# Fetching codewords by indirect DMA in place of a one-hot matmul, in a four-layer convolution kernel

## What is computed

```python
x = jnp.transpose(inputs, (0, 2, 3, 1))
flat = x.reshape(-1, 32)
distances = jnp.sum(flat * flat, axis=1, keepdims=True) + jnp.sum(codebook * codebook, axis=1) - 2.0 * flat @ codebook.T
indices = jnp.argmin(distances, axis=1)
quantized = codebook[indices].reshape(input_shape)
quantized = x + jax.lax.stop_gradient(quantized - x)
```

## Time and profile before

| | |
|---|---|
| median of 3 runs | 2005.93 us (1997.58 to 2012.52) |
| span of the profiled execution | 1997.8 us |
| busy: PE / DVE / ACT / POOL | 83% / 73% / 61% / 59% of the span |
| scoring stage of group 4 | 1034.1 to 1112.8 us |
| scoring stage of group 0 | 151.3 to 222.3 us |

### The profile page before, as it was taken

The page is one execution under the profiler, slowest core; times in us unless marked ns, Lnnn a source line. Parts: engine busy times, 40 slices in busy tenths (PEclk is TensorE's granted clock), DMA queues, the critical chain, the costliest instruction groups (busy, mean ns, idle before and its releaser), DMA issues.

```text
span 1997.8 us, 48789 instructions
## 1 busy us (share of the span) xinstructions
PE 1651.5 (83%) x18498; PEld 1357.9 (68%) x18498; DVE 1465.0 (73%) x3147; ACT 1213.4 (61%) x1819; POOL 1176.1 (59%) x1578
## 2 busy tenths in 40 slices
PE   0238657989889898888989898898989898898999
PEld 0113346668856787668856797668866797668998
DVE  3147647887779877797769777787768866797776
ACT  0003245667657675667757585666757576677986
POOL 4000036677657756577657666577657765577764
PEclk9965578999989998999989899899989998999999
DMA  8944396469755796459955696558955696235542
GB/s 146 216 112 137 82 209 172 137 172 228 201 140 182 179 221 180 143 161 225 224 149 163 168 236 194 143 160 211 217 162 145 179 229 178 62 86 144 152 143 84
DMA packets 286788, 333.16 MB, mean 167 GB/s; under 512 B 215664, under 2 KB 225904, under 8 KB 282332
## 3 DMA queue, kind: packets, MB, share of 16 engines
q1 hardware_dynamic: 240856, 228.88, 44.5%
q0 software_dynamic: 28176, 80.41, 16.5%
q10 hardware_dynamic: 17524, 20.75, 3.5%
HBM read 256.45 MB, written 60.09 MB: 158 GB/s over the span
## 4 chain that ended last, share of the span: by engine, by line
PE 52%; DVE 15%; DMA 7%; issue 6%; ACT 5%; SPq 5%; DVEq 4%; POOL 3%; ACTq 2%; POOLq 0%
PE bank L1353 28%; PE bank L1452 6%; PE bank L1340 4%; SPq L453 4%; DMA lent<-z_rows 3%; PE bank L1437 3%; DVE code L1215 3%; PE bank L1410 2%; PE bank L1337 2%; DVEq L1214 2%; PE bank L1322 2%; DVE onehot L1222 2%; PE bank L1471 2%; DMA y_patches<-yc 2%; DVE top L1213 2%
## 5 line engine op out<-in xcount | busy, mean ns | idle before, releaser
L617 POOL DMA_INDIRECT fetched<-row_pairs,corner x768 | 747.3, 973 | 520.5 <-DVE weighted L1006 318.8
L1353 PE MATMUL bank<-lent,tent 128*128 128x160 f32 x6144 | 973.9, 314 | 5.2 <-issue 2.8
L1353 PEld LDWEIGHTS bank<-lent,tent 128*128 128x128 f32 x6144 | 894.5, 199 | 110.2 <-issue 80.8
L998 DVE TENSOR_TENSOR strip<-bank,near 128x480 f32<-128x480 f32 x512 | 333.4, 652 | 204.1 <-PE bank L1353 199.4
L738 ACT ACTIVATE tent<-lent,row_at_sb 128x768 f32<-128x768 f32 x512 | 449.5, 925 | 53.2 <-PE bank L1353 36.6
L742 ACT ACTIVATE tent<-tent 128x1536 f32<-128x1536 f32 x256 | 380.0, 1484 | 20.9 <-issue 0.4
L1452 PE MATMUL bank<-cb,xs 64*128 64x512 f32 x512 | 216.3, 705 | 22.9 <-DVE code L1215 14.5
L1213 DVE MAX8 top<-bank 128x8 f32<-128x512 f32 x256 | 175.7, 687 | 38.7 <-PE bank L1452 38.6
L1012 DVE TENSOR_REDUCE samp<-strip 128x96 f32<-128x480 f32 x274 | 179.0, 653 | 25.3 <-issue 0.4
L727 ACT COPY samp_t<-bank 96x384 f32<-96x384 f32 x256 | 119.7, 468 | 101.1 <-PE bank L1340 78.3
L824 ACT COPY xs<-xn 32x128 f32<-32x128 f32 x256 | 75.6, 295 | 170.4 <-PE bank L1452 152.2
(11 more groups left out here) (148 smaller groups left out, 1429.3 us busy)
## 6 DMA issues: line engine op xcount, KB each, us to landing
lent<-z_rows SPq DMA_DIRECT2D x256, 384.0 KB
picked_weights<-arena SPq DMA_DIRECT2D x14, 1800.0 KB
arena<-picked_weights SPq DMA_DIRECT2D x21, 720.0 KB
arena<-windows SPq DMA_DIRECT2D x288, 50.0 KB
arena<-xp SPq DMA_DIRECT2D x96, 136.0 KB
fetched<-row_pairs,corner POOLq DMA_INDIRECT x768
arena<-row_pairs SPq DMA_DIRECT2D x64, 160.0 KB
slice<-picked_weights SPq DMA_DIRECT2D x14, 720.0 KB
```

The costliest lines, as they stand in the source:

```text
L617: pool.indirect_dma_start(fetched[:, N % FETCHES, k].rearrange("p q c -> p (q c)"), None, pairs_dram[b % 2], bass.IndirectOffsetOnAxis(ap= ...
L998: dve.tensor_tensor(y, STRIPS[J % 3][:, 0:DENSE * XW * C].rearrange("p (d c x) -> p d c x", d=DENSE, c=C), w.broadcast_to([128, DENSE, C, ...
L1353: m = pe.matmul(STRIPS[j % 3][:, XW * C * e:XW * C * (e + 1)], tent[:, N % TENTS, c, DENSE * d + e], picture[:, b % 2, i, c], start=(c == ...
```

## The change

The one-hot route goes: the diagonal, its spreading matmul, the copy, the compare and the 48 matmuls, with their buffers and the codebook's bf16 parts. Instead GpSimd issues one indirect DMA for every (t, i), which fetches 128 codewords from the codebook in memory by the index that VectorE has just found (`look_up`); two of them stand behind each second (t, i) in GpSimd's order. TensorE turns a tile's words, 128x128, with one transpose two tiles later (`turn_words`). Indices and words have four buffers. In the scoring stage GpSimd now sums only the first half of each tile, and VectorE the second.

```diff
+HEAVY = 4
-        for name in ("scores", "spell", "pick", "norm3", "rows", "near"):
+        ON_POOL["scores"] = (0,)
+        for name in ("spell", "pick", "norm3", "rows", "near"):
             ON_POOL[name] = (0, 1)
...
+            def look_up(g, t, i):
+                T = TILES * g + t
+                pool.wait_ge(score_read, IMG * T + i + 1)
+                if i == 0 and T >= HEAVY:
+                    pool.wait_ge(q_done, T - HEAVY + 1)
+                pool.indirect_dma_start(words[:, T % HEAVY, i, :], None, A["codebook"],
+                                        bass.IndirectOffsetOnAxis(ap=code[:, T % HEAVY, i, 0:1], axis=0)
+                                        ).then_inc(words_in[T % HEAVY], 16)
...
-                at("scores", 0, SCORE_HALVES // 2)
-                if k:
-                    pick_weights(k, 1)
-                at("scores", SCORE_HALVES // 2)
+                for t in range(TILES):
+                    for i in range(IMG):
+                        at("scores", *beside_score(t, i))
+                        if i % 2 == 1:
+                            look_up(g, t, i - 1)
+                            look_up(g, t, i)
+                    if t == TILES // 2 - 1 and k:
+                        pick_weights(k, 1)
...
                 def unit(t, i):
                     dve.wait_ge(score_done, n + 1)
+                    if i == 0 and T >= HEAVY:
+                        dve.wait_ge(words_in[T % HEAVY], 16 * IMG * (T // HEAVY))
...
-                pe.wait_ge(onehot_ready, TILES * g + t + 1)
+                pe.wait_ge(words_in[T % HEAVY], 16 * IMG * (T // HEAVY + 1))
...
+                    pe.transpose(P4[:, 128 * (t % 4):128 * (t % 4 + 1)],
+                                 words[:, T % HEAVY].rearrange("p i c -> p (i c)"), ident[:]).then_inc(q_done, 1)
```

More of the change, by code:

```diff
@@ L12 @@
 U32 = mybir.dt.uint32
-BF16 = mybir.dt.bfloat16
-F16 = mybir.dt.float16
 B, C, H, W = 32, 32, 32, 32
@@ L55 @@
 CODES = 512
-CCH = CODES // 128
+HEAVY = 4
 TILES = PIX // 128
@@ L76 @@
 MIDDLE = FAR * (NBLK - 1) / 2 + (H + 1) / 2
-PARTS = 3
 INPUTS = ["x", "Wg", "bg", "Wexp", "bexp", "w_route", "b_route", "w_mix", "codebook", "codebook_t",
           "w_grid", "b_grid", "w_conv", "ident", "gate_of", "ones",
-          "code_at", "first_rank", "grid", "row_at", "column_at"]
+          "first_rank", "grid", "row_at", "column_at"]
 def build(nc, A):
@@ L150, in build @@
         xs2 = sb("xs2", [128, 2, 128])
[L151 to L155, removed]
         top = sb("top", [128, IMG, 8])
-        code = sb("code", [128, IMG, 8], U32)
-        code_f = sb("code_f", [128, 2, IMG])
+        code = sb("code", [128, HEAVY, IMG, 8], U32)
+        words = sb("words", [128, HEAVY, IMG, C])
         q2 = arena[:, SLICE + NV * ROWN:SLICE + NV * ROWN + PIX]
@@ L252, in build @@
         score_read = sem("score_read")
[L253 to L257, removed]
+        words_in = [sem(f"words_in{u}") for u in range(HEAVY)]
         q_done = sem("q_done")
@@ L345, in _ @@
             for dst, src in (
-                (ident[:], A["ident"]), (spread[:, 0, :], A["gate_of"]), (code_at[:], A["code_at"]),
+                (ident[:], A["ident"]), (spread[:, 0, :], A["gate_of"]),
                 (ones[:], A["ones"]), (rank[:], A["first_rank"]), (grid[:], A["grid"]),
@@ L555, in _ @@
             pool.dma_start(cb2[0:C, :], A["codebook_t"]).then_inc(loaded_later, 16)
-            pool.dma_start(codes.rearrange("p (k c) -> p k c", c=C),
-                           A["codebook"].rearrange("(k p) c -> p k c", p=128)).then_inc(loaded_later, 16)
             pool.dma_start(bgrid[:], A["b_grid"].partition_broadcast(128)).then_inc(loaded_later, 16)
@@ L824, in stage @@
                     act.copy(xs2[2 * C * (i % 2):2 * C * (i % 2) + C, i // 2, :], xn2[C * i:C * (i + 1), 128 * t:128 * (t + 1)]).then_inc(staged2, 1)
[L826 to L838, removed]
                 for i in range(IMG):
@@ L847, in front @@
                         at("scores", *beside_score(t, i))
[L848 to L852, removed]
                 at("spell")
-                copy_spelt(TILES - 1)
                 at("pick")
@@ L967, in prepare @@
                 dve.tensor_tensor(g, g, bias.broadcast_to([128, 2, TILES, TAPS]), ALU.add)
[L969 to L975, removed]
                 dve.tensor_tensor(cbsq, cb2[0:C, :], cb2[0:C, :], ALU.mult).then_inc(sq_ready, 1)
@@ L1212, in unit @@
                     dve.wait_ge(score_done, n + 1)
+                    T = TILES * g + t
+                    if i == 0 and T >= HEAVY:
+                        dve.wait_ge(words_in[T % HEAVY], 16 * IMG * (T // HEAVY))
                     dve.max(top[:, i, :], SCORES[n % 2][:, :])
                     dve.drain()
[L1215 to L1223, removed]
+                    dve.max_index(code[:, T % HEAVY, i, :], top[:, i, :], SCORES[n % 2][:, :]).then_inc(score_read, 1)
                 def residual(h):
@@ L1239, in front @@
                             unit(t, i + 1)
-                        if i == IMG - 2:
-                            dve.drain()
-                            dve.tensor_copy(code_f[:, t % 2, :], code[:, :, 0]).then_inc(code_ready, 1)
                         at("scores", *beside_score(t, i))
-                        if i == 2 and t > 0:
-                            compare(t - 1)
                         if i == 2 and t == 0 and k:
@@ L1453, in scores, with turn_words @@
                               ).then_inc(score_done, 1)
[L1455 to L1462, removed]
-                    pe.wait_ge(onehot_ready, TILES * g + t + 1)
+                def turn_words(t):
+                    T = TILES * g + t
+                    pe.wait_ge(words_in[T % HEAVY], 16 * IMG * (T // HEAVY + 1))
                     if t == 0 and k:
@@ L1482, in front @@
                         if i == 0 and t > 1:
-                            pick_code(t - 2)
-                        if i == 1 and t > 0:
-                            spell(t - 1)
+                            turn_words(t - 2)
                         if i == 1 and t == 0 and k:
@@ L1489, in front @@
                             spread_gates(k)
-                pick_code(TILES - 2)
+                turn_words(TILES - 2)
                 at("spell")
-                spell(TILES - 1)
                 at("pick")
-                pick_code(TILES - 1)
+                turn_words(TILES - 1)
                 at("norm3")
@@ L1532, in _ @@
             convolve(ALL // SET - 1)
-LOADS = 16 * (11 + IMG)
-LOADS_LATER = 16 * (IMG + 5 + 3)
+LOADS = 16 * (10 + IMG)
+LOADS_LATER = 16 * (IMG + 4 + 3)
 def constants():
```

8 lines of the change are left out of this document (removed).

## The result

The change makes the kernel slower: a median of 2062.05 us (2050.13 to 2064.3) against 2001.76 us (1984.45 to 2012.52) for the kernel before, timed beside it. The ratio is 1.029, with a 95% interval of 1.023 to 1.036. The forecast was 2049 us. The profiled execution after spans 2058.7 us, 60.9 us more than the 1997.8 of before.

What follows compares the result with a forecast made beforehand. GpSimd's occupied queue was taken to become the bound beside the scores. Seven groups at +54.1 us less 10.6 in group 0 give +43.5 on the 1997.8 span, 2041; with 8.1 up to the median, 2049 us, range 1988 to 2095.

Steps and rivals of the forecast that it cites:

- A lookup at 0.98 + 0.29 = 1.27 us: Price of one indirect DMA on GpSimd's queue, instruction plus gap, taken from the fetches; 32 a group make 40.6 us.
- cheap enough: Rival: a lookup on GpSimd with its gap costs 1.08 us or less, so the kernel is not slower; chance 0.13.
- about even: Rival: a lookup costs 1.15 us with its gap and group 0 gains at its better end, 2017 us; chance 0.14.
- The queue is then occupied for ... 95.2 us: GpSimd's queue beside one scoring stage: 71.5 us before, less 16.9 for ten sums, plus 40.6 for 32 lookups.
- 1.4 us after the instruction's end: End of the scoring stage: a lookup's words land 1.4 us after its instruction ends, as a fetch's packets did.
- Group 7: Its distance from GpSimd's first fetch to `residual(1)` was set 1.9 us shorter, because it fetches no weights.
- Group 0: Its scoring stage has no layer-3 halves beside it; stage and tail were to gain 10.6 us, between 4 and 16.
- From there TensorE's `turn_samples` waits for GpSimd's sums: In the scoring stage, 9.2 us of slack is gone after four or five of ten tiles; then GpSimd sets the pace.
- VectorE and TensorE: In group 4's scoring stage VectorE's need shrinks from 78.7 to 75.7 us, TensorE's busy time from 74.2 to 68.0.
- The tail and its cover: After scoring GpSimd is about 12 us later but wins it back; if not, up to 2 us a group more.
- Words stuck behind weights: Rival: lookups queue behind 1.8 MB weight fetches on GpSimd's DMA queue; six groups pay 18 us, 2067 us; chance 0.07.
- TensorE's clock: Rival: in the paced stage TensorE's clock falls to a mean of 0.65, 10 us a group more, about 2120; chance 0.04.

## Why the prediction was right, and where its numbers were off

*Direction and mechanism: right, and shown.* GpSimd's occupied time is the bound beside the scores: three kernels with 0, 10 and 20 sums lie at 85.9, 100.2 and 118.1 us, and unread lookups alone make the kernel 10% slower. The size came out less well, and part of the fit is chance, as the sum below shows.

*A lookup at 0.98 + 0.29 = 1.27 us: right.* It took 0.967 + 9.8 / 32 = 1.27 us. Rows of 128 bytes are no cheaper than rows of 512, so the rival "cheap enough" (1.08 us) falls, and so does "about even" (1.15).

*"The queue is then occupied for ... 95.2 us": the first mis-sized term.* It measured 96.4. I took 6.4 us of gaps for 24 of the 30 fetches; the other six had ended in a wait for `weighted`, which hid their gaps. When the waits went, these gaps came out: 7.9 + 0.3 us. That is 0.27 us for each of the 30, also for those that wait today.

*"1.4 us after the instruction's end": the second, and the larger one.* The last words were turned 3.7, 3.6, 1.6, 4.0, 4.6 and 3.4 us after the lookup's end in groups 1 to 6, a mean of 3.5, +2.1 us a group. I had read the landing in a quiet stretch and not asked which loads SyncE issues there; moving these showed it. The two terms make the 97.0 us into the 100.2 of groups 1 to 6.

*Group 7.* I took off 1.9 us for the weights that it does not fetch; it came to 98.5 us instead of 95.1. One gap of 1.70 us at 1824.24 and a few long lookups (up to 1.39 us) are in its timeline. The gap stands in group 7 of three of the other kernels with ten sums and of that with 20 too (1.70 to 1.71 us); why, I did not test.

*Group 0: right.* The stage lost 8.8 us and the tail 3.5, 12.3 against a forecast of 10.6.

*The sum.* 22.6 us more in the seven groups, 1.7 more gained in group 0 and 3.5 gained outside turn the forecast span of 2041 into 2058.7. The median stands 3.4 us above this span, not 8.1, so 13 us of miss are left. The 3.5 us gained outside and the 4.7 us of the median have no part in the argument: that they made the miss smaller is luck.

*"From there TensorE's `turn_samples` waits for GpSimd's sums": the wrong line, and forecast too late.* Beside the seven stages these waits come to 1.7 us, those for words to 135.6. In group 4 the lookups trail the found index by 1.4 to 3.3 us in tile 0 and by 5.2 to 9.2 in tile 1, and TensorE waits 3.2 us for tile 1's words already. I had counted the sums' slack and left out the words' own: they are wanted two tiles behind the index. When the words were turned a tile later, the wait that I had forecast came (42.1 us), and the queue took as long.

*VectorE and TensorE: both mis-sized, at no cost.* VectorE's busy time in the stage fell by 4.2 us, where I had 3.0. TensorE's fell by 3.1 us, where I had 6.2: a transpose took 0.33 us instead of 0.2, and 60 score matmuls took 25.0 us where 61 had taken 23.3. Neither engine is the bound here.

*The tail and its cover: right.* From `residual(1)` to the next group's first fetch it takes a mean of 136.0 us in groups 1 to 6, against 137.1 before, so GpSimd's lag is won back there.

*Words stuck behind weights: there, but not the price.* TensorE does wait at tile 4 while the weights land, as that rival said. But GpSimd's queue runs on without a wait, and with tile 4's wait gone the mean distance fell by only 1.3 us. *TensorE's clock: not as that rival had it.* It was granted 0.90 to 0.94 of full speed in the stages of groups 1 to 7, against 0.96 to 1.00 before, far from the mean of 0.65 that the rival needed.

## What to carry to other kernels

Here an indirect DMA cost GpSimd's queue about 1.27 us, with rows of 128 bytes as with rows of 512. Count such instructions with their gaps against the issuing engine's slack in the very stage, not against its share of the run. When a wait on one line grows, ask first whether the pacing engine ever waits: turning the words later took away half of the largest new wait and gained nothing, and taking ten sums a group off the pacing queue moved the ratio from 1.029 to 0.984. Look in the trace whether an experiment took away what it was meant to: the shorter weight fetch left a 1.8 MB store that held the words as long. Price the two halves of such a trade apart: of the three splits tried (0, 10 and 20 sums), only that with no sums beside the scores makes the lookups pay.

## What was not expected of the hardware

VectorE's `weighted` (two inputs in SBUF) gets faster as GpSimd sums less beside it. Its mean in group 4's stage is 656 ns in the kernel before (20 sums), 573 ns after the change (10) and 546 ns with none. The trace of the kernel before says which ones are slow. Of 63 `weighted` in the scoring stages of groups 1 to 7, 25 overlap a sum and have a mean of 746 ns; the 38 others have 546, and none of them over 552.

Timelines of the kernel before, group 1: two `weighted`, and the sums that they meet.
```profile
393.33 0.87 DVE L1006 TENSOR_TENSOR weighted<-fetched,share 128x384 f32<-128x384 f32 x1
...
403.12 0.55 DVE L1006 TENSOR_TENSOR weighted<-fetched,share 128x384 f32<-128x384 f32 x1
```
```profile
393.22 0.56 POOL L650 TENSOR_TENSOR strip<-strip 128x192 f32<-128x192 f32 x1
...
403.16 0.77 POOL L656 TENSOR_TENSOR samp<-strip 128x96 f32<-128x96 f32 x1
```
The first began 0.11 us after a sum and took 0.87 us. The second began 0.04 us ahead of a sum and took its usual 0.55, and that sum took 0.77 us instead of 0.41. In these two pairs the one that began second was held up. The Trainium skill, "SBUF — State Buffer", section "SBUF: two separate sides", gives a reason: GpSimd and VectorE share one port pair as an exclusive lock, and an operation of VectorE with two inputs in SBUF meets it against a GpSimd operation that reads SBUF. These rows agree; no run isolates the lock.

Group 0's stage became 8.8 us shorter while TensorE was granted its lower level (0.50 of full speed, 1.2 GHz) throughout and was busy 55.3 of 62.2 us. Before the change it was 0.55, with TensorE busy 57.1 of 71.0 us. VectorE's busy time there fell from 55.3 to 48.2 us and ScalarE's from 20.9 to 8.3; that the stage got shorter at the lower clock because there was less to do is my reading, and why the clock fell with the one-hot matmuls gone, no run tests.
